# Six of every 64 edge tiles taken from the table by matrix products instead of gathers

## The reference

```python
h = (x @ W).reshape(n, H, C)
e = leaky_relu(a_s[src] + a_d[dst], 0.2)
p = exp(e - segment_max(e, dst)[dst])
alpha = p / segment_sum(p, dst)[dst]
out = segment_sum(h[src] * alpha[:, :, None], dst)
```

## Time and profile before

| | us |
|---|---|
| median of 3 runs | 4817.93 (4815.9 to 4823.98) |
| the profiled execution | 4823.79 |
| its span | 4822.0 |

### The profile page before, as it was taken

One profiled execution on the slowest core, in us unless ns is written; L12 is line 12 of the kernel. 1 busy time (PEld: TensorE's weight loads), 2 busy tenths in 40 slices (PEclk: granted clock), 3 DMA queues, 4 the chain that ended last, 5 costly groups with the idle time before them and its releaser, 6 DMA issues. The chain is left out here.

```text
span 4822.0 us, 44175 instructions
## 1 busy us (share of the span) xinstructions
PE 1878.0 (39%) x10326; PEld 1332.3 (28%) x10326; DVE 2816.6 (58%) x8282; ACT 651.3 (14%) x1668; POOL 2540.5 (53%) x2652
## 2 busy tenths in 40 slices
PE   0179889697132323232303232323231233323234
PEld 0133333454131313131203231313230222222222
DVE  6599999324264646464926464646482455555558
ACT  0077777200000000000000000000010000000002
POOL 4200000000777777777177777777617777777750
PEclk9999999898565656566656565656555656566666
DMA  2111111152222222222023222222203222222210
GB/s 89 42 49 73 72 48 72 42 201 116 66 68 61 68 60 67 61 67 51 7 68 70 62 70 63 70 63 70 51 12 72 61 67 61 68 61 67 61 41 14
DMA packets 123922, 307.22 MB, mean 64 GB/s; under 512 B 48180, under 2 KB 66848, under 8 KB 119971
## 3 DMA queue, kind: packets, MB, share of 16 engines
q0 software_dynamic: 84768, 176.49, 16.1%
q1 hardware_dynamic: 38914, 128.22, 7.8%
HBM read 251.37 MB, written 53.15 MB: 63 GB/s over the span
## 5 line engine op out<-in xcount | busy, mean ns | idle before, releaser
L1198 POOL DMA_INDIRECT work<-table,lane_src x2490 | 2377.9, 955 | 759.2 <-issue 753.1
L1295 PE MATMUL psum<-work 128*128 128x136 f32 x4980 | 745.0, 319 | 406.1 <-DVE work L1422 248.6
L1295 PEld LDWEIGHTS psum<-work 128*128 128x128 f32 x4980 | 724.8, 227 | 434.1 <-issue 434.1
L1343 DVE TENSOR_TENSOR work<-psum,work 128x256 f32<-128x256 f32 (+1 forms) x39 | 20.0, 514 | 1265.1 <-PE psum L1258 1265.1
L1650 POOL DMA_INDIRECT spread<-node_spread,node_pos_first x75 | 75.5, 1007 | 1255.1 <-DVEq L1575 1117.2
L1258 PE MATMUL psum<-identity,work 128*128 128x128 f32 x104 | 31.4, 432 | 1297.8 <-ACT work L1230 1297.8
L874 DVE TENSOR_SCALAR work<-iota_cols,work 128x400 f16<-128x400 f16 x1568 | 481.9, 332 | 0.0
L845 PE MATMUL psum<-work 128*128 128x448 f16 x2100 | 454.7, 355 | 11.5 <-DMA work<-counts 10.8
L1230 ACT COPY work<-work 128x64 f32<-128x64 f32 (+2 forms) x156 | 52.3, 335 | 2574.4 <-DMA work<-table,lane_src 2574.4
L1258 PEld LDWEIGHTS psum<-identity,work 128*128 128x128 f32 x104 | 16.8, 210 | 1300.1 <-issue 1087.0
L902 PE MATMUL psum<-work 128*128 128x400 f16 x1568 | 337.7, 338 | 74.2 <-DVE work L874 50.3
(11 more groups left out here) (332 smaller groups left out, 2169.6 us busy)
## 6 DMA issues: line engine op xcount, KB each, us to landing
work<-table,lane_src POOLq DMA_INDIRECT x2490, 2.5
counts<-work SPq DMA_DIRECT2D x14, 2800.0 KB, 8.5
work<-counts SPq DMA_DIRECT2D x14, 2800.0 KB
work<-spread SPq DMA_DIRECT2D x78, 256.0 KB, 4.5
work<-masks SPq DMA_DIRECT2D x78, 128.0 KB, 2.9
spread<-work SPq DMA_DIRECT2D x1, 3584.0 KB
table<-node_table SPq DMA_DIRECT2D x10, 330.0 KB, 3.0
masks<-work SPq DMA_DIRECT2D x1, 1792.0 KB, 6.7
```

What stands on the lines that cost most here:

```text
L1198: pool.indirect_dma_start(m.ring[:, s % SLOTS, 0:F + H], None, m.d_table[H], bass.IndirectOffsetOnAxis(ap=m.src[:, s:s + 1], axis=0)).then ...
L1295: mm = pe.matmul(sum_slot(u), m.onehot[b % 2][:, s % U, :], m.ring[:, s % SLOTS, :], start=(s % 2 == 0), stop=(s % 2 == 1))
```

## The change

One, the steps: units of two tiles are given up. A step is one edge tile, and there are 782 + 24 = 806 of them for each attention, still in 13 groups of 64; the last group has 38 where it had 62. Blocks have 8 steps. Each step has a PSUM slot of its own (8 steps in three banks, always the same three), and a product waits until the addition of the block before has emptied its bank.

Two, one buffer of sums: `m.acc_odd` is gone, and with it L1518 and half of the rescaling at L1404. There is one addition for each step, and each waits for the one before it. The node tile's place is kept as a row offset (tile times 136) and used on the flat buffer.

Three, aided steps: the first 6 steps of every group are not gathered. The table is kept in SBUF as three bf16 parts (high, middle, low) that add up to the f32 value; `node_stage` makes them with two more copies by ACT and two subtractions by DVE for each part of a block. For each of the 25 node tiles a one-hot of the 6 x 128 source numbers (128 x 768, bf16) is made: 17 of them by ACT in two operations, 8 by DVE in one. PE multiplies each by the three parts: 18 products of 128 x 132 (or 136) for a one-hot, 450 for a group, summed in two PSUM banks. ACT copies the result into the ring. The one-hots of the next group use a ring of five; five of them are made ahead, in the ACT program behind the copy of the result and ahead of the column copies of the next group. PE does those five in the gaps of the score part and the other twenty behind the products of the 8 blocks (3, 2, 3, 2, ...).

The diff, cut to its core:

```diff
-UNIT_TILES = EDGE_TILES // 2
-REAL_STEPS = 2 * (UNIT_TILES + NODE_TILES - 1)
-U = 16
+REAL_STEPS = EDGE_TILES + NODE_TILES - 1
+U = 8
+AIDED = 6
+HOTS = 5
+AHEAD_HOTS = 5
+PART_HOTS = (3, 2, 3, 2, 3, 2, 3, 2)
...
+    m.thirds = [m.arena[:, at + i * words:at + (i + 1) * words].bitcast(BF16).rearrange("p (j f) -> p j f", f=W) for i in range(3)]
...
             for g in range(G):
-                chain(dve.tensor_scalar(hit[:, 0:T2 - 1], begin_all[:, 0:T2 - 1], unit[:, g:g + 1], None, ALU.is_le))
+                chain(dve.tensor_scalar(hit[:, 0:T - 1], begin_all[:, 0:T - 1], step[:, g:g + 1], None, ALU.is_le))
...
+    def hot_on_dve(dve, g, hi):
+        wait_for_hot(dve, g, hi)
+        odd = lambda view: view.rearrange("p (a e) -> p a e", a=3)
+        dve.tensor_scalar(odd(hot_of(g, hi)), odd(m.aid_rows[g % 2]), m.tile_low[:, hi:hi + 1], None, ALU.is_equal).then_inc(hot_dve, 1)
...
         def _(pool):
...
+            for b in range(BLOCKS):
+                if b * U >= SLOTS:
+                    pool.wait_ge(product, min((b + 1) * U, REAL_STEPS) - SLOTS)
+                for s in gathered(b):
+                    pool.indirect_dma_start(m.ring[:, s % SLOTS, 0:F + H], None, m.d_table[H],
...
         def _(act):
+            def hot_on_act(g, hi):
+                wait_for_hot(act, g, hi)
+                away = m.aid_far[far[0] % 2]
+                act.activation(away, m.aid_rows[g % 2], ACT.Abs, bias=m.low_tile[:, hi:hi + 1]).then_inc(far_known, 1)
+                far[0] += 1
+                act.wait_ge(far_known, far[0])
+                act.activation(hot_of(g, hi), away, ACT.Relu, bias=1.0, scale=-1.0).then_inc(hot_act, 1)
+
+            def take_aided(g):
+                act.wait_ge(hot_used, (g + 1) * NODE_TILES)
...
+                for n in range(AIDED // PER_BANK):
+                    rows = slots(g * GROUP + n * PER_BANK, PER_BANK)[:, :, 0:F + H]
+                    act.copy(rows, m.ps[3][:, n * 512:n * 512 + PER_BANK * W].rearrange("p (s f) -> p s f", f=W)[:, :, 0:F + H]).then_inc(aid_taken, 1)
...
                 act.copy(slots(g * GROUP, GROUP)[:, :, F:W], ps_coef.rearrange("p (h s) -> p s h", s=GROUP)).then_inc(tails, 1)
+                if g + 1 < GROUPS:
+                    for hi in range(AHEAD_HOTS, NODE_TILES):
+                        if hi not in by_dve:
+                            hot_on_act(g + 1, hi)
+                    take_aided(g + 1)
+                if g + 2 < GROUPS:
+                    for hi in range(AHEAD_HOTS):
+                        hot_on_act(g + 2, hi)
...
         def _(pe):
+            def aid(g, his):
...
+                for hi in his:
+                    pe.wait_ge(hot_dve if made_by_dve(g, hi) else hot_act, made(g, hi))
...
+                    for part, third in enumerate(m.thirds):
+                        for k in range(AIDED):
+                            mm = pe.matmul(ps_aid[k], hot_of(g, hi)[:, k * P:(k + 1) * P], third[:, hi, 0:F + H],
...
+                    mm.then_inc(hot_used, 1)
...
                 t.then_inc(scores_turned, 1)
+                aid(g + 1, range(0, 2))
...
+                aid(g + 1, range(2, 3))
...
+                aid(g + 1, range(3, AHEAD_HOTS))
...
                     for s in steps_of(b):
...
+                        if s % U % PER_BANK == 0 and s >= U:
+                            pe.wait_ge(summed, bank_end(s - U))
+                        pe.matmul(sum_slot(s), m.onehot[b % 2][:, s % U, :], m.ring[:, s % SLOTS, :],
+                                  start=True, stop=True).then_inc(product, 1)
+                    aid(g + 1, part_of[b * U % GROUP // U])
...
             def add_up(b):
...
+                for k, s in enumerate(steps_of(b)):
...
+                    at = dve.snap(m.j_regs[k % REGS], min_val=0, max_val=LAST_ROW)
+                    if k % PER_BANK == 0:
+                        dve.wait_ge(product, bank_end(s))
+                    if s:
+                        dve.wait_ge(summed, s)
+                    to = sums[:, bass.ds(at, W)]
+                    dve.tensor_tensor(to, to, sum_slot(s), ALU.add).then_inc(summed, 1)
...
                 for b in blocks_of(g):
                     message(b)
                     onehot(b)
+                    if g + 1 < GROUPS:
+                        hot_on_dve(dve, g + 1, part_of[b * U % GROUP // U][-1])
                     if b > blocks_of(g)[0]:
                         add_up(b - 1)
...
-    chain(dve.tensor_tensor(acc[:, :, 0:used], acc[:, :, 0:used], odd[:, :, 0:used], ALU.add))
...
+            def rest(b):
+                dve.wait_ge(high_taken, len(parts) * (b + 1))
...
+                    dve.tensor_tensor(product, product, high[:, j, :], ALU.subtract).then_inc(rest_known, 1)
+
+            def lowest(b):
+                dve.wait_ge(middle_taken, len(parts) * (b + 1))
...
+                    dve.tensor_tensor(low[:, j, :], out_part(b, n)[:, :, 0:F + H], middle[:, j, :], ALU.subtract).then_inc(thirds_known, 1)
```

More of the change, by code:

```diff
@@ L176, in allocate @@
     at += 2 * U * P
-    m.raw = [m.arena[:, at + h * 8 * P:at + (h + 1) * 8 * P] for h in range(2)]
-    at += 16 * P
+    m.raw = m.arena[:, at:at + 8 * P]
+    at += 8 * P
     words = len(MASKS) * P // 2
@@ L321, in step_tables @@
 def step_tables(nc, m, a):
-    T, T2 = EDGE_TILES, UNIT_TILES
+    T = EDGE_TILES
     rows = [m.big[:, i * T:(i + 1) * T] for i in range(6)]
@@ L326, in step_tables @@
     at = 6 * T
-    unit, odd, t_of, j_of, j_cap, unit_i, odd_i = (m.big[:, at + i * G:at + (i + 1) * G] for i in range(7))
-    at += 7 * G
+    step, t_of, j_of, j_cap = (m.big[:, at + i * G:at + (i + 1) * G] for i in range(4))
+    at += 4 * G
     ones = m.big[:, at:at + P]
@@ L350, in _ @@
             pe.wait_ge(dve_step, 5)
-            for row, out, n in ((begin, ps_begin, T2), (last_f, ps_last, T)):
+            for row, out, n in ((begin, ps_begin, T), (last_f, ps_last, T)):
                 for lo in range(0, n, 512):
@@ L1152, in attend @@
     counted = m.ps[1][:, 3 * P:4 * P]
+    ps_aid = [m.ps[3][:, t // PER_BANK * 512 + t % PER_BANK * W:][:, 0:F + H] for t in range(AIDED)]
     SPREAD, AHEAD, BACK = range(3)
@@ L1586, in _ @@
                 b = wave - last - 1
-                if self_loops and b >= 0:
-                    scores(b)
+                if 0 <= b < TURNS:
+                    if self_loops:
+                        scores(b)
+                    rest(b)
+                if b >= 1:
+                    lowest(b - 1)
+            dve.wait_ge(thirds_known, len(parts) * TURNS)
         @block.tensor
@@ L1599, in _ @@
                 pe.wait_ge(copied, b + 1)
-                if b >= (2 if w_res is None else 1):
-                    pe.wait_ge(tables, per_block * (b - (1 if w_res is None else 0)))
+                if b >= 1 and w_res is not None:
+                    pe.wait_ge(tables, per_block * b)
+                if b >= 2:
+                    pe.wait_ge(thirds_known, len(parts) * (b - 1))
                 for k in range(BLK):
@@ L1610, in _, with middles @@
         def _(act):
+            def middles(b):
+                act.wait_ge(rest_known, len(parts) * (b + 1))
+                for n, (lo, hi) in enumerate(parts):
+                    j = slice(b * BLK + lo, b * BLK + hi)
+                    act.copy(middle[:, j, :], out_part(b, n)[:, :, 0:F + H]).then_inc(middle_taken, 1)
             for wave in range(TURNS + last):
```

267 lines of the change are left out of this document (163 added, 104 removed).

## The result

The change makes the kernel faster by 4.6%: 4598.72 us (median of 4 runs, 4597.01 to 4601.48) beside 4817.86 us for the kernel before, ratio 0.9544, 95% interval 0.9527 to 0.956. The direction of the forecast (4710 us) was right and its size only half: 219 us were gained where 108 were forecast.

What follows compares the result with a forecast made beforehand. The chain of the other engines, DVE in the blocks and ACT behind them, replaces GpSimd as bound; attentions -127 us, outside +20, so -107 from 4823.8: 4717, as a median 4710 us, range 4570 to 4880 (this case's own span 4640 to 4790).

Steps and rivals of the forecast that it cites:

- the sum of the chain: One group's period outside GpSimd, from score start to score start: 76.4 us with 4 heads, 79.8 with 8, both over 72.8.
- addition, start to start: DVE's addition of one step, each waiting for its predecessor with one buffer: 0.43 us, twice as many of them.
- one-hot on DVE, in three pieces: DVE's one-hot of 768 elements in a block: 0.50 us, since the view in three pieces may cost the fast rate.
- bf16 product with its load, in blocks: PE's product of 132 columns with weight load: 0.07 us, between 0.056 and 0.1155; on average 45 a block, 3.15 us.
- piece B: First message to last product of a group, the eight blocks, paced by DVE: 47.0 us.
- piece A: Score start to first message of a group: 14.6 us with 4 heads, 17.6 with 8.
- piece C: Last product to next score, with ACT's aided copy, five one-hots, then column copies: 14.8 us, 15.2 with 8 heads.
- rival 2: GpSimd stays the bound, additions 0.33 us or one-hots cheaper: period 72.8 to 75, total 4540 to 4640 us; chance 0.17.
- the floor: GpSimd's own time for the 58 gathers of a group, 58 x 1.256 = 72.8 us.
- Rival 3: PE becomes the bound of the blocks, from 0.093 us a bf16 product on: 4840 to 5040 us; chance 0.28.
- The lock on GpSimd's descriptors: DVE's eight one-hots in a two-port mode could cost GpSimd up to 2.7 us a group, 75.5 for 72.8.
- Outside: Outside the attentions: 30 us of DVE subtractions less 13.0 for L1518, 5 us for counted steps, together +20 us.

Runs made afterwards that it cites:

- gathers56: The changed kernel with two more gathers of each group left out, their steps keeping the rows in their slots: 4561.18 us, ratio 0.9474.
- onehot_twice_b: The changed kernel with DVE's one-hot of each block made twice, the second after a wait for the first: 4839.31 us, ratio 1.0053.
- one_part: The changed kernel with only the first of the three bf16 parts multiplied, 6 products for a one-hot instead of 18: 4589.29 us, ratio 0.9534.
- columns_first: The changed kernel with ACT's column copies of the next group ahead of the five one-hots: 4570.79 us, ratio 0.9493.
- steps_only: The changed kernel without aided rows, all 64 rows of a group gathered, single-tile steps and one buffer kept: 4821.22 us, ratio 1.0012.

## Why the prediction was right and wrong

**Right: the frame.** Six gathers fewer, a hidden chain that comes to the surface (with 8 heads), three pieces of it, DVE the bound of the blocks with PE under it, ACT's five one-hots in C. `gathers56`, `onehot_twice_b`, `one_part` and `columns_first` show the links.

**Wrong: the terms of the chain, nearly all on the dear side.** The step that failed is the sum of the chain: "Both are over 72.8, so the chain and no longer GpSimd sets the period". The forecast had 76.4 us with 4 heads; the pieces measure 71.7 and the period 73.0, set by the gathers. Over 12 periods that is 41 of the 45 and 47 us by which these attentions were missed. With 8 heads the chain does bound, but 79.8 was forecast and 76.7 measured, 37 of 42 us. Term by term:

| term | forecast | measured |
|---|---|---|
| addition, start to start | 0.43 | 0.42 to 0.43 |
| one-hot on DVE, in three pieces | 0.50 | 0.33 |
| bf16 product with its load, in blocks | 0.07 | 0.061 |
| f32 products of a block | 1.85 | 2.07, the next product 1.91 behind the first |
| block on DVE | 6.2 | 6.0 |
| piece B | 47.0 | 45.2 and 45.7 |
| piece A | 14.6 and 17.6 | 12.9 and 16.9 |
| two copies, pair of one-hots on ACT | 1.1 and 1.72 | 0.88 and 1.70 |
| column copies | 1.7 | 1.2 |
| piece C | 14.8 and 15.2 | 13.6 and 14.4 |

The addition, which decided between forecast and rival 2, was read rightly out of a gap of 0.15 between two operations at register addresses. Two terms carry most of the miss. In B it is the one-hot: the rows for 128 and 400 elements gave 0.34 from start to start, and the forecast went to 0.50 because the view in three pieces might lose the fast rate. It doesn't (8 x 0.17 = 1.4 us of B's 1.8). In A the forecast added 1.5 us for aided products in the way of the maxima and the drop. At the maxima DVE waits 0.96 us (ahead of L1479) where it waited 0.56 before. At the drop it is the other way, first in the kernel before, then in the change:

```profile
2057.21 0.57 PE L1273 MATMUL psum<-work,select_columns 128*128 128x2 f32 x2
...
2057.89 0.16 DVE L1391 TENSOR_SCALAR rescale_ratio<-psum 128x4 f32<-128x4 f32 x1 [0.62 <-PE psum L1273]
```

```profile
1808.79 0.36 PE L1391 MATMUL psum<-work,select_columns 128*128 128x2 f32 x2
...
1809.48 0.16 DVE L1507 TENSOR_SCALAR rescale_ratio<-psum 128x4 f32<-128x4 f32 x1
```

The wait of 0.62 us is gone, since the small products of the drop run right behind aided ones at a granted clock of 1.00, where it was 0.50 before (with 8 heads it falls from 1.15 to 0.34 in most groups); in `steps_only` and in `one_part` it is back. So A is 12.9, under even the 13.2 that the forecast had for "all hidden". In C each term was a little high. No term was off by much; all but the f32 products lean the same way, and over 36 periods 3.3 us are 119.

**Wrong: the floor, in the other direction.** The forecast had the chain over GpSimd everywhere. With 4 heads it lies under it, so these attentions are rival 2's (989 forecast there, 989.3 and 986.8 measured), and the total lies in its span of 4540 to 4640 and not in the forecast's own, 4640 to 4790. Its reason was the one-hot or the addition: the one-hot held, at 0.17 us a block, and the addition didn't, so its block of 5.4 us and B of 41 are wrong (6.0 and 45.2); that its 989 is met to the microsecond is luck. With 8 heads rival 2 had 1015 and 1036.6 came, between it and the forecast's 1079. Its chance of 0.17 was too small beside 0.50: the forecast's period sat 3.6 us over a hard floor with nearly all terms rounded up. One of its signs failed with the floor: GpSimd was to wait several us a group for a product, and waits 13.7 us in 39 groups, since it runs ahead into the ring.

**Rival 3 (PE becomes the bound)** is refuted: 0.061 us, and `one_part` gains 0.7 us a period for 30 products less in each block. The Trainium skill (TensorE: Matmul & The Clock Gate, Back-to-back issue gap) gives about 81 ns for 128 columns with their weight load; this trace, with 54 in 3.27 us at 132 columns, stands under it, so the measurement decides.

**The lock on GpSimd's descriptors**, which the Trainium skill (SBUF — State Buffer, SBUF: two separate sides) states for VectorE's two-port modes, would have cost up to 2.7 us a group by the forecast's sum. In attention 1 a gather comes every 915.7 / 727 = 1.2596 us with eight one-hots in each group and every 1009.8 / 805 = 1.2544 without them: 0.3 us for 58, part of it waits for products (in `one_part`, with the same eight, it is 1.2555). By that sum 2.4 us more should show; the trace doesn't bear it out here, and whether these one-hots run in such a mode no run shows.

**Outside.** The forecast's +20 came out as +38, of which 37 are the register loads of the count list and only 1 the rest. Neither part was seen: the three bf16 parts were costed at 10 us in each stage and hide almost wholly (stage 1 unchanged at 64.6 us, stage 2 and 3 some 3 us each once L1518's 4.3 are set against them), and that data was moved under code that the change doesn't touch was priced at nothing, not even named. These two errors, about 20 us too much and 37 too little, partly hid each other in the total.

## What to carry to other kernels

When a chain and a fixed floor lie within a few us of each other, cost the chain with the likeliest value of each term and keep the caution for the range; then give the floor the chance that the terms' common lean leaves it. Shortening the bound engine's work pays only until the last group: with few gathers left there, the chain of the group before it sets the end. And a diff that moves a small tensor under unchanged code has changed that code: look at what reads it, register loads above all, and at the offset it now has.

## What the runs showed of the hardware

- A register load of eight numbers by DVE took 0.60 us, and of four 0.34, from a tensor of its own or from a multiple of 16 bytes of the big buffer; 8 bytes behind such a multiple it took 1.84 and 0.96, and 6.2 to 6.4 where it met a 2.8 MB store, until the store's traffic was over. Beside the same store the shifted load took 1.24. The profile calls the idle time of the engine issue, since no semaphore ends it.
- The register load of 0.60 us ahead of the additions stood bare behind a wait, with 0.47 us of idle time, that it didn't cost where it ran beside earlier operations.
- The granted clock follows the work that the change adds. Windows of 200 us of the first attention, with 6 aided rows a group and with none (length, busy and count of PE, PEld, DVE, ACT, POOL, then the clock):

```profile
1700.00:1900.00 200.00, 139.02 (x1586) 128.49 (x1584) 150.81 (x378) 89.51 (x134) 151.63 (x159) 0.85 0.31 70
```

```profile
1700.00:1900.00 200.00, 92.45 (x410) 80.27 (x411) 137.26 (x327) 8.89 (x31) 151.24 (x161) 0.59 0.28 64
```

  With the aided products the clock is at 0.85 on average, 0.94 within the blocks, and 16 f32 products of a block take 2.07 us at 1.00 (2.4 GHz). Without them it is at 0.59 and the same 16 take up to 3.97, at 0.50 (1.2 GHz; at 1880.18 of `steps_only`). In `one_part` it is 0.73. So 1176 more products in the window add only 47 us of busy time on PE.
